# Edge scores of a graph network on one core: target rows spread by one-hot products in a new stage before the scoring stage, part of the source rows gathered there

## The chip, the core and the metric

The kernel runs on one core of a Trainium2 chip. The metric is the time of one launch on the device in microseconds (us). The core has a matrix engine (TensorE, PE; its weight loads are listed apart as PEld), a vector engine (VectorE, DVE), a scalar engine (ScalarE, ACT), a general engine (GpSimd, POOL), a sequencer that only issues transfers (SyncE, SP), and 16 DMA engines that all queues share.

## The reference, cut to what matters

x has 50,000 nodes of 128 values; there are 50,000 edges with a source and a target. The edges are sorted by target; sources are random. Four graph layers follow one another, each with a residual and a layer norm. The change is in the fourth:

```python
q = (node_features @ Wq.T + bq).reshape(N, H, D)
k = (node_features @ Wk.T + bk).reshape(N, H, D)
v = (node_features @ Wv.T + bv).reshape(N, H, D)
scores = jnp.sum(q[src] * k[dest], axis=-1) / jnp.sqrt(jnp.float32(D))
scores = scores + attention_mask
seg_max = jax.ops.segment_max(scores, src, num_segments=N)
ex = jnp.exp(scores - seg_max[src])
seg_sum = jax.ops.segment_sum(ex, src, num_segments=N)
weights = ex / seg_sum[src]
weighted = v[src] * weights[:, :, None]
out = jax.ops.segment_sum(weighted, dest, num_segments=N)
```

## The kernel before, in words

Nodes and edges are cut into 392 tiles of 128 rows each, and these into 98 groups of four tiles (Q = 4). A table of a group in HBM is 256 KB. `program` runs the stages one behind the other, with a barrier of all engines between them (`end_phase`, L63): `setup` (L68), the edge MLP, an aggregation `agg0`, `normalise_project`, the aggregations `agg1` to `agg4` (of which `agg1` to `agg3` run node work beside them), `project_normalise`, then `edge_scores` (L1645), `softmax_by_source` (L1978), `agg5` and a last `project_normalise`.

**An aggregation** (`aggregate`, L269) adds the rows of edges into the rows of their targets. Since edges are sorted by target, it walks 784 steps (node tiles and edge tiles merged), four steps to a quad, 196 quads. For each quad VectorE makes four one-hot tiles in one instruction (L450), and TensorE multiplies each with a tile of edge rows into a bank of PSUM (L520); ScalarE empties a finished bank (L562, L564), fills it with its start values (L551, L553) and stores it. The numbers of steps at which buffers come free are worked out in `setup` and read into registers as the stage runs.

**agg1** has `MeanProducts` (L651) beside it: for each finished group its sums are read back and TensorE transposes them (`turn`, L722) and multiplies them with two weights (`products`, L731 to L737). VectorE's step for a group (L772) does first `keep` of the group four before (L758: copy of the first product, L763: second product plus a residual), then `copy` of the group two before (L770: transposed rows from PSUM). TensorE's `turn` of a group waits for that copy, since there are two transposed buffers.

**edge_scores** handles one group of 512 edges at a time:

- POOL gathers four tiles of source rows and four of target rows of `x3` (`gather`, L1718, one indirect DMA of 128 rows of 512 B at L1737 for each tile), and three groups later scatters four tiles of scores by source (`scatter`, L1742, L1748). It also copies indices (L1716). These are 12 indirect DMAs for a group, all issued in order by POOL.
- TensorE transposes the eight tiles (`turn`, L1776 and L1777), transposes the group's one-hot rows (`lean`, L1786), starts the products of the previous group with their biases (L1808, L1809), then for each of four tiles looks up a place in the order of sources (`look_up`, L1797 and L1798) and does the products of the previous group (L1812, L1813); at last it counts (L1819).
- ScalarE rounds the table of places (L1859), copies the transposed source rows from PSUM (L1852), copies the transposed one-hot rows (`copy_lo`, L1866) and keeps two products of the previous group (L1875, L1876).
- VectorE copies the transposed target rows from PSUM (`copy_target`, L1911), forms the rest of the rounding (L1939), then in turns a rank (L1945) and the selection from the looked up row (L1950) for each of the four tiles, writes the places (L1954 to L1960), scores the previous group (L1916 to L1924) and makes the one-hot rows of the next group (`make_hot`, eight instructions at L1932 and L1933).
- SP loads a row of 512 source numbers, broadcast to 128 partitions (L1696), and stores the group's values (L1701).

The look-up of a tile waits for the selection of the tile before (L1796), and the selection waits for the look-up (L1949), so that the two engines hand over to each other four times in a group. The order of the work on each engine is the order in its `body`.

## Time and profile before

| | |
|---|---|
| median of 3 runs | 7013.81 us (7011.34 to 7027.35) |
| the profiled execution | 7010.85 us |
| its span, first to last instruction | 7009.2 us |
| mean granted TensorE clock, share of full | 0.793 |
| instructions | 133354 |
| moved by DMA | 1119.21 MB |

A row of the view of windows gives for a stretch the busy time of each engine with its count of instructions, the granted clock, the mean busy share of the 16 DMA engines and the rate in GB/s. A row of the view of groups gives line, engine, operation, output and input, count, busy time and mean ns of one, then the time that the engine was idle before them and what ended that. A fp32 matmul of this kernel stands in the trace as two MATMUL records.

### The profile page before, as it was taken

To read this page: it belongs to the slowest core of one execution; us is meant where nothing else is said; L and a number is where in the kernel's file an instruction comes from. 1 tells how busy PE (TensorE), PEld (TensorE's weight loads), DVE (VectorE), ACT (ScalarE), POOL (GpSimd) and SP (SyncE) were. 2 spreads that over 40 slices of the span, in tenths; PEclk is the share of its full clock that TensorE was granted. 3 is DMA by queue.
4 is the path that set the end of the run, shared out by engine and by line. 5 is a ranking of instruction groups with operands and counts; after the bars stand their busy time and mean duration, and the time that the engine had idled before them with its cause. 6 is when DMAs were issued, how large, how long until landed. Compare 5 with 4: busy or idle time off the path is not lost. (4 is left out here: it accounts for less than half of the span.)

```text
span 7009.2 us, 133354 instructions
## 1 busy us (share of the span) xinstructions
PE 4774.6 (68%) x26165; PEld 3739.8 (53%) x26166; DVE 4285.0 (61%) x13848; ACT 2451.2 (35%) x6084; POOL 4258.3 (61%) x4642
## 2 busy tenths in 40 slices
PE   3666666778868876546887767666666666346557
PEld 2555555557757765435764555444444444235545
DVE  4555556887635543863556757866666666665458
ACT  1555555325652125205313416711111111122149
POOL 3777773003575557667776775477777777347730
PEclk7777777999989988558999967977777777667579
DMA  1222223658969976976875536722222222123358
GB/s 29 72 75 73 74 73 110 196 168 297 342 207 302 314 253 210 343 247 207 268 227 180 179 96 232 248 74 69 70 72 69 69 72 69 49 81 115 85 181 289
DMA packets 616834, 1119.21 MB, mean 160 GB/s; under 512 B 124786, under 2 KB 133392, under 8 KB 616336
## 3 DMA queue, kind: packets, MB, share of 16 engines
q1 hardware_dynamic: 299984, 547.66, 23.3%
q10 hardware_dynamic: 183456, 334.05, 13.8%
q0 software_dynamic: 133280, 236.29, 12.7%
q8 instruction: 34, 0.56, 0.0%
q14 instruction: 80, 0.66, 0.0%
HBM read 675.98 MB, written 441.55 MB: 159 GB/s over the span
## 5 line engine op out<-in xcount | busy, mean ns | idle before, releaser
L520 PE MATMUL agg_bank<-agg_msgs,agg_onehot 128*128 x7840 | 1344.0, 325 | 541.9 <-DVE agg_onehot L450 423.6
L520 PEld LDWEIGHTS agg_bank<-agg_msgs,agg_onehot 128*128 128x128 f32 x7840 | 1161.7, 227 | 777.2 <-issue 773.1
L450 DVE TENSOR_TENSOR agg_onehot<-iota,rel 128x512 f32<-128x512 f32 x1176 | 809.9, 689 | 706.6 <-PE agg_bank L520 271.3
L368 POOL DMA_INDIRECT agg_msgs<-near,agg_rows x784 | 792.7, 1011 | 375.3 <-issue 205.5
L368 POOL DMA_INDIRECT agg_msgs<-y,agg_rows x784 | 784.6, 1001 | 261.6 <-issue 200.4
L564 ACT ACTIVATE agg_kept<-agg_bank 128x512 f32<-128x512 f32 x294 | 175.6, 597 | 1097.9 <-PE agg_bank L520 1084.0
L365 POOL DMA_INDIRECT agg_weight<-weights,agg_rows x392 | 410.7, 1048 | 124.4 <-issue 103.0
L520 PE MATMUL agg_bank<-agg_weighted,agg_onehot 128*128 x1568 | 339.5, 387 | 209.9 <-DVE agg_onehot L450 161.8
L1452 POOL DMA_INDIRECT mlp_xs<-in_x,mlp_rows x392 | 409.2, 1044 | 116.7 <-issue 115.8
L562 ACT ACTIVATE agg_kept<-agg_bank,inv_root 128x128 f32<-128x128 f32 x784 | 224.1, 369 | 721.2 <-PE agg_bank L520 672.1
L1748 POOL DMA_INDIRECT by_source<-score_line,score_places x392 | 389.3, 993 | 125.6 <-issue 117.4
L1060 POOL TENSOR_SCALAR l_o<-l_z,l_rstd,l_shift 128x128 f32<-128x128 f32 x196 | 85.7, 440 | 610.8 <-DVE l_shift L1105 608.4
L1776 PE MATMUL score_pSrc<-ident,score_xs 128*128 128x128 f32 x392 | 149.8, 392 | 449.9 <-issue 326.6
L1452 POOL DMA_INDIRECT mlp_xd<-in_x,mlp_rows x392 | 385.7, 984 | 116.0 <-issue 112.1
L1737 POOL DMA_INDIRECT score_xd<-x,score_rows x392 | 384.6, 981 | 116.1 <-issue 116.1
L1737 POOL DMA_INDIRECT score_xs<-x,score_rows x392 | 380.0, 969 | 116.6 <-issue 110.5
L520 PEld LDWEIGHTS agg_bank<-agg_weighted,agg_onehot 128*128 128x128 f32 x1568 | 294.1, 281 | 255.8 <-issue 255.8
L1950 DVE CUSTOM_DVE_ANT_0 score_look_sink<-score_look,score_hot_hi 128x392 f32<-128x392 f32 x392 | 222.1, 567 | 270.6 <-PE score_look L1798 268.3
L1472 PE MATMUL mlp_pSrc<-ident,mlp_xs 128*128 128x128 f32 x392 | 140.1, 372 | 342.4 <-DMA mlp_xd<-in_x,mlp_rows 296.5
L1776 PEld LDWEIGHTS score_pSrc<-ident,score_xs 128*128 128x128 f32 x392 | 77.6, 198 | 485.1 <-issue 485.0
L1812 PE MATMUL score_pQV<-score_w_qv,score_xsT 128*128 128x256 f32 x784 | 333.3, 519 | 0.0
L527 PE MATMUL agg_counts<-agg_hot_hi,agg_hot_lo 128*128 128x392 bf16 x784 | 216.9, 362 | 150.0 <-issue 77.3
(344 smaller groups left out, 11942.3 us busy)
## 6 DMA issues: line engine op xcount, KB each, us to landing
sums<-agg_kept ACTq DMA_DIRECT2D x490, 256.0 KB
agg_first<-start ACTq DMA_DIRECT2D x196, 256.0 KB
agg_first<-y ACTq DMA_DIRECT2D x196, 256.0 KB
messages<-mlp_m SPq DMA_DIRECT2D x98, 256.0 KB, 2.1
agg_first<-in_x ACTq DMA_DIRECT2D x98, 256.0 KB
agg_msgs<-messages SPq DMA_DIRECT2D x98, 256.0 KB
l_z<-sums SPq DMA_DIRECT2D x98, 256.0 KB
x<-l_o POOLq DMA_DIRECT2D x98, 256.0 KB
```

The costliest lines, as they stand in the source:

```text
L365: pool.indirect_dma_start(weight[:, j, :], None, weights[:, :], bass.IndirectOffsetOnAxis(ap=rows[:, third, j:j + 1], axis=0)).then_inc(sm ...
L368: pool.indirect_dma_start(msgs[:, j, :], None, table[:, :], bass.IndirectOffsetOnAxis(ap=rows[:, third, j:j + 1], axis=0)).then_inc(sm[f"g ...
L450: nc.vector.tensor_tensor(onehot[:, j, :, :], k.iota[:, 0:P].unsqueeze(1).to_broadcast([P, Q, P]), k.rel[:, ds(i * (4 * Q) + j * Q, Q)].un ...
L520: t.matmul(bank[:, column[q], :], onehot[:, j, q, :], messages[:, slot[q], :], start=False, stop=True, skip_group_check=True)\
L527: last = t.matmul(counts[:, 0:NT], hot_lo[:, j, w, :], hot_hi[:, j, w, :], start=False, stop=True, skip_group_check=True)
L562: last = a.activation(kept[:, u, q, :], bank[:, u * Q + q, :], ACT.Relu if floor else ACT.Copy, scale=scale[:, ds(g * Q + q, 1)])
L1452: pool.indirect_dma_start(to[:, b, q, :], None, x[:, :], bass.IndirectOffsetOnAxis(ap=rows[:, half, which, at + q:at + q + 1], axis=0)).th ...
L1737: pool.indirect_dma_start(to[:, b, q, :], None, x3[:, :], bass.IndirectOffsetOnAxis(ap=rows[:, half, which, at + q:at + q + 1], axis=0)).t ...
L1748: pool.indirect_dma_start(by_source[:, :], bass.IndirectOffsetOnAxis(ap=places[:, b, q:q + 1], axis=0), line[:, b, q, :], None).then_inc(s ...
L1776: t.transpose(pSrc[:, q, :], xs[:, u, q, :], k.ident[:, :])
L1812: t.matmul(pQV[:, q, :], xsT[:, u % 2, q, :], w_qv[:, :], start=False, stop=True, skip_group_check=True)
L1950: v.tensor_tensor_reduce(out=look_sink[:, q, :], in0=look[:, 0:NT], in1=hot_hi[:, u % 2, q, :], scale=1.0, scalar=0.0, op0=ALU.mult, op1=A ...
```

## The change

`setup` also transposes the table of each step's relative edge targets and writes it to HBM as bf16 rows (seven transposes, two copies, one DMA).

A new stage `spread_rows` runs before `edge_scores`. It walks the same 196 quads as an aggregation, the other way round: SP loads node tiles of `x3` in order (98 loads of 256 KB), VectorE compares the broadcast relative rows with the partition's number to make the one-hot tiles, TensorE multiplies them with the node tiles, so that each edge gets its target's row, and ScalarE empties each finished group of edges, clears the bank and stores 256 KB to `target_rows`. POOL issues 49 broadcast loads of the relative rows (one for four quads, 512 KB each, two buffers) and, between them, gathers the source rows of every fourth group (24 groups, 96 indirect DMAs) and stores them to `source_rows`.

In `edge_scores` SP loads the target rows of each group from `target_rows`, and the source rows of each fourth group from `source_rows`; POOL gathers sources for the other three only, and no targets. The copy of the transposed target rows moves from VectorE to ScalarE, behind the copy of the source rows.

In `MeanProducts` VectorE's `copy` (lag 2) moves ahead of `keep` (lag 4).

The diff, cut to its core and with its indentation shortened:

```diff
+    sp.wait_ge(sm["rel_rows"], 2)
+    sp.dma_start(rel_rows.rearrange("a (j s e) -> s (a j) e", s=REL_ROWS, e=P), relT[:, :, :]).then_inc(sm["rel_out"], 16)
+    sp.wait_ge(sm["rel_out"], 16)
...
+    dve.wait_ge(sm["turned_rel"], STEPS // REL_ROWS)
+    v.tensor_copy(relT[:, 0:4, :], pT[0:REL_ROWS, :, :]).then_inc(sm["rel_rows"], 1)
+    v.tensor_copy(relT[:, 4:7, :], pHT[0:REL_ROWS, 0:3, :]).then_inc(sm["rel_rows"], 1)
...
+    pe.wait_ge(sm["pe_ready"], 6)
+    for j in range(STEPS // REL_ROWS):
+        to = pT[0:REL_ROWS, j, :] if j < 4 else pHT[0:REL_ROWS, j - 4, :]
+        t.transpose(to, k.rel[:, j * REL_ROWS:(j + 1) * REL_ROWS], k.ident[:, :]).then_inc(sm["turned_rel"], 1)
...
-for lag, what in ((4, keep), (2, copy)):
+for lag, what in ((2, copy), (4, keep)):
...
+def spread_rows(nc, k, table, rel_rows, out, ahead):
+
+    ROUNDS = (GROUPS - BANKS) // BANKS
...
+        nodes = sb("nodes", [P, RING, C])
+        rel = sb("rel", [P, 2, CHUNK, Q * P], BF16)
+        onehot = sb("onehot", [P, CHUNK, Q, P])
+        kept = sb("kept", [P, BANKS, Q, C])
+        zero = sb("zero", [P, Q, C])
+        rows, got = sb("rows", [P, 2, Q], I32), sb("got", [P, 2, Q, C])
+        bank = ctx.enter_context(nc.psum_tensor("spread_bank", [P, BANKS * Q, C], F32))
...
+    def store(i, m):
+        pool.wait_ge(sm[f"moved{m}"], i * (16 * Q) + 16 * Q)
+        pool.dma_start(rows_of(ahead, i * (2 * DEEP) + (m * DEEP + DEEP - 1)), got[:, m, :, :]).then_inc(sm[f"kept{m}"], 16)
+
+    def gather(i, m):
+        if not isinstance(i, int) or i > 0:
+            pool.wait_ge(sm[f"kept{m}"], i * 16)
+        pool.sem_inc(sm["pass_pool"], 1)
+        pool.wait_ge(sm["rows"], i * 2 + (m + 1))
+        pool.sem_inc(sm["pass_pool"], 1)
+        for q in range(Q):
+            pool.indirect_dma_start(got[:, m, q, :], None, table[:, :], bass.IndirectOffsetOnAxis(
+                ap=rows[:, m, q:q + 1], axis=0)).then_inc(sm[f"moved{m}"], 16)
+
+    def chunk(i, c):
+        if not isinstance(i, int) or i * CHUNK + c >= 2:
+            pool.wait_ge(sm["onehot"], i * (CHUNK * CHUNK) + (c - 1) * CHUNK)
+        pool.sem_inc(sm["pass_pool"], 1)
+        pool.dma_start(rel[:, c % 2, :, :], rel_rows[:, ds(i * (CHUNK * CHUNK * Q * P) + c * (CHUNK * Q * P), CHUNK * Q * P)]
+                       .to_broadcast([P, CHUNK * Q * P])).then_inc(sm[f"rel{c % 2}"], 16)
+
+    def body(i):
+        for c in range(CHUNK):
+            chunk(i, c)
+            if c % 2 == 0:
+                copy_rows(i, c // 2)
+            else:
+                gather(i, c // 2)
+                if c == 3:
+                    store(i, 0)
+                elif not isinstance(i, int) or i > 0:
+                    store(i - 1, 1)
...
+    def load(i, u):
+        g = i * DEEP + u
+        sp.wait_ge(sm["summed"], sp.value_load(k.node_left[0:1, ds(g, 1)], min_val=1, max_val=STEPS + SHIFT))
+        sp.dma_start(nodes[:, u * Q:(u + 1) * Q, :], rows_of(table, g)).then_inc(sm[f"loaded{u}"], 16)
+
+    def arrive(i, u):
+        sp.wait_ge(sm[f"loaded{u}"], i * 16 + 16)
+        sp.sem_inc(sm["arrived"], 1)
+
+    def body(i, u):
+        for lag, step in ((0, load), (2, arrive)):
+            if live(*before_by(i, u, lag)):
+                step(*before_by(i, u, lag))
+
+    rounds(sp, body, 2)
...
+        dve.wait_ge(sm[f"rel{c}"], i * 16 + 16)
+        for j in range(CHUNK):
+            at = i * (2 * CHUNK) + (c * CHUNK + j)
+            ready = dve.snap(least[0], min_val=1, max_val=ET)
+            arrived = dve.snap(least[1], min_val=1, max_val=GROUPS)
+            dve.sem_inc(sm["pass_dve"], 1)
+            dve.wait_ge(sm["arrived"], arrived)
+            dve.sem_inc(sm["pass_dve"], 1)
+            dve.wait_ge(sm["ready"], ready)
+            dve.sem_inc(sm["pass_dve"], 1)
+            dve.wait_ge(sm["summed"], i * (2 * CHUNK * Q) + ((c * CHUNK + j) * Q + 1))
+            nc.vector.tensor_scalar(onehot[:, j, :, :], rel[:, c, j, :].rearrange("p (q e) -> p q e", q=Q), k.pid[:, 0:1], None, ALU.is_equal)\
+              .then_inc(sm["onehot"], 1)
+            read_needs(ds(at + 1, 1))
...
+    with pe.Fori(0, CHUNKS) as i:
+        for j in range(CHUNK):
+            column = [pe.snap(r, min_val=0, max_val=BANKS * Q - 1) for r in regs[0:Q]]
+            slot = [pe.snap(r, min_val=0, max_val=RING - 1) for r in regs[Q:2 * Q]]
+            pe.wait_ge(sm["onehot"], i * CHUNK + (j + 1))
+            for q in range(Q):
+                t.matmul(bank[:, column[q], :], onehot[:, j, q, :], nodes[:, slot[q], :], start=False, stop=True, skip_group_check=True)\
+                 .then_inc(sm["summed"], 1)
+            for half in (0, Q):
+                pe.reg_load(regs[half:half + Q], k.places[0:1, ds(i * CHUNK + (j + 1), 1), half:half + Q])
...
+        act.wait_ge(sm["summed"], act.value_load(k.edge_done[0:1, ds(g, 1)], min_val=1, max_val=STEPS + SHIFT))
+        a.activation(kept[:, u, :, :], bank[:, u * Q:(u + 1) * Q, :], ACT.Copy).then_inc(sm["emptied"], 1)
+        act.wait_ge(sm["emptied"], g + 1)
+        if not isinstance(i, int) or g + BANKS < GROUPS:
+            fill(u)
+        act.dma_start(rows_of(out, g), kept[:, u, :, :]).then_inc(sm[f"written{u}"], 16)
...
+    def load_rows(i, u):
+        g = i * DEEP + u
+        if after(i, u, DEEP):
+            sp.wait_ge(sm["turned"], g - (DEEP - 1))
+            sp.sem_inc(sm["pass_sp"], 1)
+        sp.dma_start(xd[:, u, :, :], rows_of(target_rows, g)).then_inc(sm[f"dst{u}"], 16)
+        if u == DEEP - 1:
+            sp.dma_start(xs[:, u, :, :], rows_of(source_rows, g)).then_inc(sm[f"src{u}"], 16)
...
-        for lag, step in ((0, load_sources), (3, store)):
+        for lag, step in ((0, load_rows), (0, load_sources), (3, store)):
...
-        for which, to, sem in ((0, xs, "src"), (1, xd, "dst")):
-            for q in range(Q):
-                pool.indirect_dma_start(to[:, b, q, :], None, x3[:, :], bass.IndirectOffsetOnAxis(
-                    ap=rows[:, half, which, at + q:at + q + 1], axis=0)).then_inc(sm[f"{sem}{b}"], 16)
-                if q == 1 and to_copy:
-                    copy_rows(g + 2, 1 - half, which, to_copy)
+                was, place = before_by(i, u, DEEP, TWICE)
+                if live(was, place, TWICE):
+                    pool.wait_ge(sm[f"src{b}"], (was * 2 + place // DEEP) * (16 * Q) + 16 * Q)
+                    pool.sem_inc(sm["pass_pool"], 1)
+        for q in range(Q):
+            pool.indirect_dma_start(xs[:, b, q, :], None, x3[:, :], bass.IndirectOffsetOnAxis(
+                ap=rows[:, half, at + q:at + q + 1], axis=0)).then_inc(sm[f"src{b}"], 16)
+            if q == 1 and to_copy:
+                copy_rows(g + 2, 1 - half, to_copy)
...
-            if live(*before_by(i, u, lag, TWICE), TWICE):
+            if live(*before_by(i, u, lag, TWICE), TWICE) and (lag or u % DEEP < DEEP - 1):
...
-        pe.wait_ge(sm[f"src{u}"], i * (16 * Q) + 16 * Q)
-        pe.wait_ge(sm[f"dst{u}"], i * (16 * Q) + 16 * Q)
+        pe.wait_ge(sm[f"src{u}"], i * (16 * Q) + 16 * Q if u < DEEP - 1 else i * 16 + 16)
+        pe.wait_ge(sm[f"dst{u}"], i * 16 + 16)
...
+        a.activation(xdT[:, u % 2, :, :], pDst[:, :, :], ACT.Copy).then_inc(sm["copied_dst"], 1)
...
-    def copy_target(i, u):
-        g = i * DEEP + u
-        dve.wait_ge(sm["turned"], g + 1)
-        if after(i, u, 2):
-            dve.wait_ge(sm["product"], g - 1)
-        v.tensor_copy(xdT[:, u % 2, :, :], pDst[:, :, :]).then_inc(sm["copied_dst"], 1)
...
+        spread_rows(nc, k, x3, rel_rows, target_rows, source_rows)
+        edge_scores(nc, k, ins, x3, source_rows, target_rows, values, by_source)
```

## Rows read from the trace of the kernel before

**Rows 1.** The page's first part: busy time and share of each engine over the span.
```profile
PE 4774.6 (68%) x26165; PEld 3739.8 (53%) x26166; DVE 4285.0 (61%) x13848; ACT 2451.2 (35%) x6084; POOL 4258.3 (61%) x4642
```

**Rows 2.** Windows: agg0, normalise_project, the middle of agg1, edge_scores.
```profile
1187.00:1604.00 417.00, 310.06 (x1959) 214.72 (x1960) 346.33 (x980) 115.52 (x194) 0.00 (x0) 0.99 0.57 180
...
1620.00:1880.00 260.00, 257.64 (x1948) 219.82 (x1949) 196.42 (x1046) 197.30 (x474) 134.60 (x287) 0.98 1.00 371
2200.00:2500.00 300.00, 263.30 (x1981) 226.50 (x1980) 177.15 (x275) 41.82 (x122) 169.53 (x181) 1.00 0.95 315
...
4531.00:6056.00 1525.00, 1031.11 (x4215) 716.89 (x4215) 968.78 (x3251) 253.06 (x490) 1164.16 (x1226) 0.72 0.25 71
```

**Rows 3.** Groups by line, edge_scores, 4700 to 5900 us.
```profile
L1748 POOL DMA_INDIRECT by_source<-score_line,score_places x310 | 307.9, 993 | 94.5 <-issue 88.4 <-DVE score_line L1924 6.1
L1737 POOL DMA_INDIRECT score_xd<-x,score_rows x310 | 303.9, 980 | 91.8 <-issue 91.8
L1737 POOL DMA_INDIRECT score_xs<-x,score_rows x312 | 302.3, 969 | 92.4 <-issue 88.1 <-PE score_pDst L1777 4.3
...
L1933 DVE TENSOR_SCALAR score_hot_hi<-iota,src_hi 128x392 bf16<-128x392 f32 x308 | 140.1, 455 | 0.0
```

**Rows 4.** Waits, edge_scores, 4700 to 5900 us: total us, times, longest us.
```profile
DVE score_xdT L1911 <- PE score_pDst L1777: 150.1, 69, 3.6
```

**Rows 5.** Timeline of VectorE, one group: start us, duration us, instruction, idle before.
```profile
5008.84 0.62 DVE L1933 TENSOR_SCALAR score_hot_hi<-iota,src_hi 128x392 bf16<-128x392 f32 x1
5009.38 0.67 DVE L1911 COPY score_xdT<-score_pDst 128x512 f32<-128x512 f32 x1
...
5012.25 0.57 DVE L1950 CUSTOM_DVE_ANT_0 score_look_sink<-score_look,score_hot_hi 128x392 f32<-128x392 f32 x1 [1.47 <-PE score_look L1798]
...
5014.18 0.57 DVE L1950 CUSTOM_DVE_ANT_0 score_look_sink<-score_look,score_hot_hi 128x392 f32<-128x392 f32 x1 [0.95 <-PE score_look L1798]
...
5016.12 0.57 DVE L1950 CUSTOM_DVE_ANT_0 score_look_sink<-score_look,score_hot_hi 128x392 f32<-128x392 f32 x1 [0.82 <-PE score_look L1798]
...
5017.34 0.57 DVE L1950 CUSTOM_DVE_ANT_0 score_look_sink<-score_look,score_hot_hi 128x392 f32<-128x392 f32 x1
...
5022.85 0.58 DVE L1933 TENSOR_SCALAR score_hot_hi<-iota,src_hi 128x392 bf16<-128x392 f32 x1
5026.17 0.69 DVE L1911 COPY score_xdT<-score_pDst 128x512 f32<-128x512 f32 x1 [2.74 <-PE score_pDst L1777]
```

**Rows 6.** Windows of 4 us in the same group: the clock is the third number from the end.
```profile
5012.00:5016.00 4.00, 4.00 (x14) 3.17 (x14) 2.09 (x8) 0.00 (x0) 2.93 (x4) 0.50 0.17 49
...
5020.00:5024.00 4.00, 0.00 (x0) 0.00 (x0) 3.24 (x11) 0.00 (x0) 3.08 (x4) 0.91 0.58 168
```

**Rows 7.** Timeline: TensorE's weight loads for one quad, in agg5.
```profile
6331.12 0.97 PEld L520 LDWEIGHTS agg_bank<-agg_weighted,agg_onehot 128*128 128x128 f32 x8 [0.35 <-issue]
```

**Rows 8.** Groups by line and form: VectorE in agg0, and at the start of edge_scores.
```profile
L461 DVE TENSOR_SCALAR agg_hot_hi<-iota,dst_hi 128x392 bf16<-128x392 f32 x392 | 163.7, 418 | 0.0
...
L1899 DVE TENSOR_SCALAR score_earlier<-iota,score_rank 128x512 f32<-128x512 f32 x4 | 1.9, 486 | 0.1
```

**Rows 9.** DMA issues: KB each, median us to landing; and one line's issue cost on POOL.
```profile
score_src_row<-in_src_rows SPq DMA_DIRECT2D x98, 256.0 KB, 4.0
...
L1067 POOL DMA_DIRECT2D x<-l_o x95 | 55.1, 580 | 0.0
```

**Rows 10.** agg1: timeline of one transpose on TensorE, and the wait's total, 2200 to 2500 us.
```profile
2306.47 0.66 PE L722 MATMUL l1p_pT<-ident,l1p_h 128*128 128x128 f32 x4 [0.49 <-DVE l1p_hT L770]
...
PE l1p_pT L722 <- DVE l1p_hT L770: 36.5, 69, 0.7
```

**Rows 11.** Timeline: VectorE's last two instructions of setup.
```profile
93.32 1.16 DVE L239 SCALAR_TENSOR_TENSOR rel<-ns,pN 128x392 f32<-128x392 f32 x2 [8.86 <-PE pN L265]
```

**Rows 12.** The join before agg0: the MLP's last work, and agg0's first quad.
```profile
1176.09 1.28 ACT L1561 ACTIVATE mlp_m<-mlp_h,ew 128x128 f32<-128x128 f32 x4 [0.28 <-DVE mlp_h L1628]
...
1187.44 1.78 PEld L520 LDWEIGHTS agg_bank<-agg_msgs,agg_onehot 128*128 128x128 f32 x8 [5.41 <-issue]
```

117 lines of the change are left out of this document (98 added, 19 removed).

## The prediction

> **What bounds the kernel now.** I read the page's first part first: over the whole span no engine is full, PE is busy 68%, POOL and DVE 61% each [rows 1]. These are averages over stages with different limits, so the view of windows comes next, one row for each stage that the change touches [rows 2]. edge_scores lasts 1525 us; POOL is busy 1164 us of it, DVE 969, PE 1031 at a clock of 0.72, and the DMA engines a quarter. The view of groups tells what POOL does there: three kinds of indirect DMA of 0.97 to 0.99 us, each with about 0.30 us of issue before it and almost no wait for another engine [rows 3]. Twelve in a group make 12 x 1.28 = 15.4 us, and 98 x 15.4 = 1509 us: POOL's queue paces this stage.
>
> The question is then what is next behind POOL. The view of waits says that DVE waits for the transposed targets 150 us in 1200, which is 1.9 us for each of the 78 groups [rows 4]. So POOL is late by little. The timeline of DVE shows it in one group [rows 5]. Take as the mark the end of the last one-hot instruction. It falls at 5009.46 (5008.84 + 0.62). The gathers were early here: the copy of the targets follows at once. The mark of the next group falls at 5023.43 (5022.85 + 0.58). This group took 13.97 us with no delay by POOL in it. Behind that mark the gathers are late: DVE idles 2.74 us. So POOL's pace of 15.4 stands over a chain between DVE and PE of about 13.9 us. That chain has three parts: 2.8 us from the mark to the first selection (5012.25), 5.1 us from the first to the fourth selection (5017.34), 6.1 us to the next mark. In the middle part PE is busy without a gap at a granted clock of 0.50, and selections come 1.93 us apart; the last comes 1.22 us behind its predecessor, when the clock has risen. In the last part PE does nothing for 4 us [rows 5, 6].
>
> **The change part by part.** All sums are against the profiled execution (7010.85 us), 3 us under the median shown.
>
> Scoring stage. POOL keeps 3 gathers on average and 4 scatters, 7 x 1.28 = 9.0 us a group, well under the chain. It no longer sets the pace. The chain of 13.9 remains. The copy of the targets leaves DVE (0.67 us), but it stood in the first part, where DVE idles 1.47 us afterwards for PE's look-up: only the idle time grows, and I count nothing. If PE's clock were full there, that cover would be thinner, and up to 0.6 us of it would show. The same copy on ACT costs 0.6 us; ACT is free then, since the transposes now come right behind the counting and some 3 us before the mark. The one-hot instructions get a little shorter: 455 ns beside a busy POOL [rows 3], 418 ns beside an idle one [rows 8]; with the small one of each pair some 0.2 us a group at most, of which I take 0.1, as POOL is still busy two thirds of the time. That makes 13.8 us. SP's queue gets one or two loads of 256 KB for a group, ahead of the source numbers and the store. Their waits are for events three groups back, so I count nothing; the DMA share of 0.25 leaves room. Without that cover each late load would stop the transposes for its landing, 4.0 us for one of this size [rows 9]. Sum: the stage's time beside its groups is 1525 - 1509 = 16 us; 98 x 13.8 + 16 = 1368, so **-157 us**. Bounds for a group: 13.5 and 14.2, for -186 and -117.
>
> The Trainium skill's page "Advanced Engine Details and Errata" (VectorE Performance Modes) says that POOL's instructions and DVE's two-port modes block each other. By that rule the new stage's one-hot instruction, of such a form and beside gathers, could wait out a POOL instruction. The trace shows 37 ns of such a cost in a mean of 455 [rows 3, 8], so the measurement decides, and I price it by that.
>
> The new stage. It walks 196 quads, with no predecessor in the trace; four resources bound it. PE: eight weight loads for a quad take 0.97 us, with 0.35 us of issue ahead where registers are read between quads [rows 7]: 1.32 us, 259 us in all. DVE: one instruction of 512 columns, about 0.49 us [rows 8], and the register reads; not the bound. POOL: for 16 quads 8 gathers of 1.28, four broadcast loads and two stores of 0.58 each [rows 9] and two copies, about 14 us, or 0.9 a quad. DMA: relative rows 49 x 512 KB, nodes in and edge rows out 98 x 256 KB each, gathers in and out 6.3 MB each, 89.7 MB together; at 371 GB/s, the rate of the stage whose DMA share is 1.00 [rows 2], 242 us. Three of these bounds are close to each other (259, 242, 176), and each load of relative rows has one chunk of four quads to land in, while POOL stands in four gathers half of the time. So it won't reach the highest of them. The nearest thing measured is agg0, same skeleton without gathers: 417 us, 2.13 a quad, but there DVE is busy 83% with five instructions [rows 2]. I take 1.45, nearer to PE's bound than to agg0, since DVE has one instruction in place of five. 196 x 1.45 = 284. Between stages lie some 10 us from the last work to the first quad [rows 12], and at the end stores land and engines meet; I add 20 for both: **+304 us**. Bounds: 242 + 20 = 262, and agg0's pace, 417 + 20 = 437.
>
> Setup. After the last instructions, which end at 94.5 us [rows 11], there now come seven transposes, two copies of about 0.7 us and a DMA of 200 KB whose landing is waited for, 2 to 4 us: **+7 us**, bounds 4 and 12.
>
> agg1. In its middle a step takes 300 / 69 = 4.35 us, and PE waits 0.5 us in each for DVE's copy, which stands behind `keep`, which in turn waits for PE's products [rows 10]. With the copy first that wait has no cause. What is late next is DMA: its share is already 0.95 at 315 GB/s [rows 2], and the highest share of rows 2 is 1.00. So a gain of 5% of the 420 us in which this pattern holds, not 0.5 / 4.35 of it: **-21 us**, bounds 0 and -45.
>
> Sum: -157 + 304 + 7 - 21 = +133, and 7010.85 + 133 = **7143 us**. The gathers that go cost less than they look: they stood over a chain that is nearly as long.
>
> **The rivals.**
>
> *The clock stays up (faster).* In the scoring stage PE waits less for data, so it could hold full speed through the look-ups. For it: the clock does rise within the look-ups, and a selection then follows after 1.22 us. Against: 4 us of idle PE in each group come from DVE's scoring and one-hot instructions, not from POOL, and they stay; the group of rows 5, which had no wait for POOL, ran its look-ups at 0.50. Price: the middle part falls from 5.1 to about 4.1 us (1.4 for each of three), the first part from 2.8 to about 1.9, so 98 x 1.9 = 186 us less: 6957 us. It decides if the granted clock of the stage goes above 0.95. The Trainium skill's page "TensorE: Matmul & The Clock Gate" (HAM oscillation) has the rule: idle gaps bring the clock back to half, and work packed without gaps keeps it up. By that rule fewer waits for gathers speak for this rival and the remaining gap against it.
>
> *The new stage goes at the pace of its relative rows (slower still).* One load of 512 KB can start only when the one-hots of the chunk before last are done. From there to the next such point lie its issue (0.6), its landing and four one-hots with their register reads (about 3.2). With two chunks in flight, 8 quads at 1.45 are 11.6 us, so it decides where landing takes over 7.8 us; half that size lands in 4.0 with the DMA engines a quarter busy [rows 9], and the gathers and a store can put up to 5.8 us in front. Price: 1.8 us a quad, 196 x 0.35 = 69 us more, 7212 us; at agg0's pace 7276.
>
> *Scoring is no shorter.* If SP's in-order queue holds back the loads, or another chain sets in at 15.4 us, nothing of the 157 comes: 7300 us. Nothing in the waits speaks for it.
>
> **How the numbers follow.** My forecast gets 0.62, the relative rows 0.21, the clock 0.10, scoring no shorter 0.04; 0.03 is left for a small miss towards no change. A measurement of this kernel can tell about 0.3% (21 us) from no change. The bounds of the forecast itself: the low ends together make -186 + 262 + 4 - 45 = +35, the high ends -117 + 437 + 12 = +332. Not all ends come together, so the range goes from 7050 to 7270, which leaves out the clock rival, the last one, and the far end of the second. Faster has the clock rival and a little more, 0.11; within 0.3% 0.03; slower 0.86.
>
> **What the profile after would show.** Right: a new stretch of about 300 us before edge_scores with the clock near 1.00, DMA share over 0.85, PE busy about 80%; edge_scores at 1370 us with POOL busy some 50% and waits of POOL for PE or DVE, selections still 1.9 us apart at a clock of 0.50, DVE idle before the first selection up by 0.6 us; agg1's middle at 4.1 us a step and no wait of PE for the copy at L770's place. Wrong: groups of edge_scores under 12.5 us would break the chain that I put at 13.9; DVE waits for relative rows in the new stage, and quads of over 1.7 us, would move me to the second rival; under 1.2 us a quad the issue time that I counted for PE was hidden.

## The result, and the profile after

| | before | changed |
|---|---|---|
| median, runs on one chip | 7012.58 us (4 runs) | 7288.88 us (7287.15 to 7290.68, 4 runs) |
| ratio | | 1.0387, 95% interval 1.0373 to 1.0401 |
| span of the profiled execution | 7009.2 us | 7289.0 us |
| instructions | 133354 | 142209 |
| moved by DMA | 1119.21 MB | 1209.10 MB |

The changed kernel is 3.9% slower. The forecast was 7143 us with 7050 to 7270 as its range: right in its direction, 146 us too low, and above the range.

The account needs the length of each stage. I take it from barrier to barrier (the instruction of `clear_and_free_semaphores` that ends each stage). Stages that are not listed moved by 4 us or less each.

| stage, us | before | changed | difference | predicted |
|---|---|---|---|---|
| setup | 95.0 | 102.4 | +7.4 | +7 |
| agg1 | 662.1 | 658.0 | -4.1 | -21 |
| new stage | | 445.3 | +445.3 | +304 |
| edge_scores | 1533.4 | 1360.7 | -172.7 | -157 |
| all others | 4718.7 | 4722.6 | +3.9 | 0 |
| sum | 7009.2 | 7289.0 | +279.8 | +133 |

Of the miss of 147 us, 141 lie in the new stage. The gain of the change, 173 us, came as forecast, and 16 us more; agg1 gave 17 us less than forecast, and it is luck that these two cancel.

The view of windows of the changed kernel, for the middle of agg1, the new stage and edge_scores (columns as in [rows 2]):
```profile
2200.00:2500.00 300.00, 281.15 (x2043) 236.94 (x2042) 174.87 (x281) 44.02 (x128) 171.08 (x185) 0.99 0.97 324
4530.00:4985.00 455.00, 301.09 (x1572) 261.36 (x1572) 101.22 (x211) 119.84 (x203) 143.38 (x197) 0.77 0.63 200
4985.00:6340.00 1355.00, 953.56 (x4215) 648.00 (x4215) 886.03 (x3140) 306.87 (x588) 688.62 (x710) 0.75 0.26 79
```
In the new stage nothing is full: PE 66%, POOL 32%, VectorE 22%, the DMA engines 0.63 at 200 GB/s. A stage where nothing is full waits in turns, or is paced by something that is not counted as busy. The waits of the stage:
```profile
ACT spread_kept L1819 <- PE spread_bank L1802: 314.0, 98, 8.6
POOL spread_rel L1709 <- DVE spread_onehot L1774: 240.5, 45, 10.5
PEld spread_bank L1802 <- issue: 176.6, 170, 6.2
DVE spread_onehot L1774 <- PE spread_bank L1802: 160.5, 102, 4.1
DVE spread_onehot L1774 <- SPq L1742: 97.0, 49, 4.3
...
PE spread_bank L1802 <- DVE spread_onehot L1774: 58.0, 51, 5.3
DVE spread_onehot L1774 <- ACT spread_bank L1812: 57.7, 28, 4.3
...
DVE spread_onehot L1774 <- DMA spread_rel<-rel_rows: 5.9, 1, 5.9
```
Three readings. ACT, POOL and DVE all wait, and most of their waits lead to PE: ACT waits for it, POOL for DVE, and DVE more for PE (160.5 us) than for SyncE's report (97.0) or ACT (57.7). PE waits 58.0 us for DVE's one-hot tiles, but its weight loads wait 176.6 us for "issue", which is no other engine. The relative rows were late once, for 5.9 us: the rival that had them set the pace is refuted. The groups of the stage give the prices:
```profile
L1774 DVE TENSOR_SCALAR spread_onehot<-spread_rel,pid 128x512 f32<-128x512 bf16 x196 | 97.4, 497 | 337.6 <-PE spread_bank L1802 160.5 <-SPq L1742 97.0 <-ACT spread_bank L1812 57.7
...
L1709 POOL DMA_DIRECT2D spread_rel<-rel_rows x47 | 26.0, 553 | 241.4 <-DVE spread_onehot L1774 240.5 <-issue 1.0
```
The one-hot instruction takes 0.497 us (0.49 priced), so it doesn't wait out POOL's gathers, and POOL's issue of a broadcast load takes 0.553 (0.58 priced). These were right.

**What fills "issue".** The timeline of the weight loads, in the changed kernel (start, duration of the eight loads of a quad, idle time before them in brackets):
```profile
4704.84 1.69 PEld L1802 LDWEIGHTS spread_bank<-spread_nodes,spread_onehot 128*128 128x128 f32 x8 [0.97 <-issue]
4706.74 1.74 PEld L1802 LDWEIGHTS spread_bank<-spread_nodes,spread_onehot 128*128 128x128 f32 x8 [0.21 <-issue]
4709.19 0.97 PEld L1802 LDWEIGHTS spread_bank<-spread_nodes,spread_onehot 128*128 128x128 f32 x8 [0.71 <-issue]
```
From start to start lie 1.90 and 2.45 us. At 4706.74 the idle time is only 0.21, because the eight loads before it took 1.69 us, at a granted clock of 0.66 in that stretch (4704 to 4707 us); at the full clock they take 0.97, and at 0.50 1.78 (e10 below, 4702 to 4704 us). So the idle time shrinks when the loads are slow, and the distance of the starts does not. The trace also has the records of PE's own sequencer, the part that issues its instructions, which the profile doesn't count as busy (start us, us, line, instruction; same stretch, the weight loads between them left out):
```
4707.10 0.074  L1802 FUSED_REGOPS    (last of four matmuls with addresses from registers)
4707.25 0.051  L1805 FUSED_REGOPS
4707.36 0.335  L1805 TENSOR_LOAD     (slots' registers: four values)
4707.75 0.051  L1805 FUSED_REGOPS
4707.86 0.914  L1805 TENSOR_LOAD     (columns' registers: four values)
4708.83 0.173  L1798 FUSED_REGOPS
```
Between two quads the sequencer issues four matmuls, about 0.16 us apart, and then two loads of registers one behind the other, each 0.50 us from start to start where it isn't held up (the second one here is). That makes 4 x 0.16 + 2 x 0.50 + 0.23 for the addresses of the next quad = 1.87 us. Over the stage's 195 distances between quads 5% are under 1.85 us, a quarter under 1.87, half under 2.10, and the mean is 2.22. Every fourth distance has a turn of the loop in it; of these half are under 2.56 us, so a turn adds about 0.68 us. A floor of 196 x 1.87 + 49 x 0.68 = 400 us is thus the stream of instructions itself; 196 x 2.22 = 435 leaves 35 us for waits, and 10 us are the joins.

### The profile page after: what moved, and what is told of

It is laid out like the page before. It is cut to its first block and busy times, and to the rows that moved or that the text cites. A ratio compares the mean times of both kernels' runs of the same rounds, so it can differ in the third digit from the quotient of the medians.

```text
span 7289.0 us, 142209 instructions
## 1 busy us (share of the span) xinstructions
PE 5019.4 (69%) x27744; PEld 3939.5 (54%) x27745; DVE 4299.5 (59%) x13952; ACT 2620.4 (36%) x6378; POOL 3924.8 (54%) x4322
## 2 busy tenths in 40 slices
DMA packets 659861, 1209.10 MB, mean 166 GB/s; under 512 B 125570, under 2 KB 134176, under 8 KB 659360
## 5 line engine op out<-in xcount | busy, mean ns | idle before, releaser
L1802 PE MATMUL spread_bank<-spread_nodes,spread_onehot 128*128 x1568 | 299.2, 354 | 140.0 <-issue 80.4
L1802 PEld LDWEIGHTS spread_bank<-spread_nodes,spread_onehot 128*128 128x128 f32 x1568 | 260.9, 252 | 179.0 <-issue 176.6
L1941 POOL DMA_INDIRECT score_xs<-x,score_rows x296 | 289.9, 979 | 87.4 <-issue 86.5
L1989 PE MATMUL score_pLo<-score_ident_b,score_hot_lo 128*128 128x128 bf16 x392 | 59.3, 306 | 374.3 <-DVE score_hot_hi L2130 374.3
```

The costliest lines, as they stand in the source:

```text
L1802: t.matmul(bank[:, column[q], :], onehot[:, j, q, :], nodes[:, slot[q], :], start=False, stop=True, skip_group_check=True)\
L1941: pool.indirect_dma_start(xs[:, b, q, :], None, x3[:, :], bass.IndirectOffsetOnAxis(ap=rows[:, half, at + q:at + q + 1], axis=0)).then_inc ...
```

## The experiments

Theory A: TensorE's sequencer paces the new stage by its loads of registers. Rivals: the gathers or the DMA traffic in the stage; the report of arrived rows by SyncE; the banks; the clock, which is 0.77 in the stage. For edge_scores: the chain of 13.7 us is what remains, and the clock sets its length.

The runs went in five sessions, each with its own runs of the kernel before. In two of them (e1 to e4, and e9 to e12) it takes 7011 to 7019 us, as above; in three (e5 to e8, f1 to f4, and f5 and f6) it takes 8258 to 8276 us. I call these the first and the second kind of session. The expectations speak of chips like the first and like the second, but that the chip makes the difference isn't shown: the record has the chips 6 and 3 for the first kind, and 12, 15 and again 6 for the second. The new stage is alike in both: 445.3, 443.1, 441.4 and 442.1 us in the first, 443.7 and 443.7 in the second, where nothing in it was changed.

**One load instead of two (e1).**
```diff
-for half in (0, Q):
-    pe.reg_load(regs[half:half + Q], k.places[0:1, ds(i * CHUNK + (j + 1), 1), half:half + Q])
+pe.reg_load(regs, k.places[0:1, ds(i * CHUNK + (j + 1), 1), 0:2 * Q])
```


> The changed kernel, but TensorE's sequencer reads the eight place registers of the next quad with one load in place of two of four. Theory A (the new stage goes at the pace of TensorE's sequencer: between the matmuls of two quads it makes two register loads of about 0.5 us each, in series): the quad of 2.2 us gets shorter by up to 0.5 us where nothing else is late, the stage of 445 us goes to 350 to 400. Theory B (the pace is set by VectorE's own waits and register load): under 10 us less. Theory C (DMA or relative rows): no change.

Measured: 7239.23 us; the new stage 392.8 us, 52.5 less; edge_scores 1360.3. The weight loads of e1:
```profile
4703.97 0.97 PEld L1802 LDWEIGHTS spread_bank<-spread_nodes,spread_onehot 128*128 128x128 f32 x8 [1.16 <-issue]
4705.73 0.97 PEld L1802 LDWEIGHTS spread_bank<-spread_nodes,spread_onehot 128*128 128x128 f32 x8 [0.79 <-issue]
4707.37 0.97 PEld L1802 LDWEIGHTS spread_bank<-spread_nodes,spread_onehot 128*128 128x128 f32 x8 [0.67 <-issue]
```
A quarter of the distances are now under 1.64 us, 5% under 1.60, some 0.24 less: one load of eight registers stands 0.76 us in the stream, two of four 1.00. A turn of the loop adds 0.49 us where it added 0.68. Together that is 196 x 0.24 + 49 x 0.19 = 56 us, near the 52.5 measured. Nothing else in the stage was touched.

**Twice the loads (e2), then four loads of two registers (e10, and e5).** In e2 each load stood twice, with `for half in (0, Q, 0, Q)`.

> The changed kernel with each of the two register loads on TensorE made twice (same values). Theory A: 1.0 us more for each quad, the stage goes from 445 to about 620 to 645 us, and nothing else moves. Theories B and C: TensorE has slack of its own, so less than half of that: under 540 us.

Measured: 7297.02 us, the stage 443.1. The trace still has two TENSOR_LOADs for a quad: 394 in the stage, as many as in the changed kernel. The repeated loads, which had no effect on any value, are not among the records. The run tells nothing of theory A. The next one keeps every load alive:
```diff
-for half in (0, Q):
-    pe.reg_load(regs[half:half + Q], ...)
+for part in range(0, 2 * Q, 2):
+    pe.reg_load(regs[part:part + 2], k.places[0:1, ds(i * CHUNK + (j + 1), 1), part:part + 2])
```


> The changed kernel, with the eight registers of a quad (four slots, four columns) fetched on TensorE in the new stage by four loads of two registers in place of two loads of four; the same eight values, none of them left out. Theory A (TensorE's own instruction stream paces the stage, and loads of registers are served one after the other at about 0.5 us each, whatever their size): two further loads, 196 x 2 x 0.5 = about +195 us if every one lay on the path, +150 to +195 us since some 45 us of the stage are other waits that a longer period covers; the new stage at about 600 to 640 us where it was 445.3, the whole at about 7440 to 7485 us. Theory B (loads are served by bytes, or the idle of the weight loads comes from the one-hot products, the banks or the rows): the new stage stays at 445 +- 10 us. All other stages unchanged in both.

> Four loads of two registers in the new stage, beside the changed kernel on one chip this time (e5 stood alone on its chip). Theory A (TensorE's instruction stream paces the stage): e5 showed a shortest period of 3.70 us a quad where the changed kernel has 1.87; 196 x 3.7 + 49 x 0.5 = 750 us, so the stage at 740 to 790 us on either chip, +300 to +330 us. Rival B (loads are not on the path and e5's stage was long by its chip): the stage within 20 us of the changed kernel's on the same chip.

Measured: the stage takes 789.9 us in e5 (second kind) and 790.9 in e10 (first kind; the whole 7630.57 us against 7287.62 for the changed kernel in the same session). The weight loads of e10:
```profile
4702.02 1.78 PEld L1802 LDWEIGHTS spread_bank<-spread_nodes,spread_onehot 128*128 128x128 f32 x8 [1.91 <-issue]
4705.72 1.78 PEld L1802 LDWEIGHTS spread_bank<-spread_nodes,spread_onehot 128*128 128x128 f32 x8 [1.92 <-issue]
4710.05 1.78 PEld L1802 LDWEIGHTS spread_bank<-spread_nodes,spread_onehot 128*128 128x128 f32 x8 [2.55 <-issue]
```
The distance is 3.70 us. Each load of two registers stands 0.71 us in the stream: 4 x 0.71 - 2 x 0.50 = 1.84, and 3.70 - 1.87 = 1.83. The granted clock also fell, to 0.50 in e10's stage (0.77 in the changed kernel's, 0.89 in e1's), but it doesn't set the distance: the eight weight loads end 1.78 us after their start, and the records of the four register loads fill the stream up to 3.34 us after it. With e1, this shows theory A: the same eight registers, in one, two or four loads, and the stage follows the number of loads in both directions, by 0.24 and 1.83 us a quad. My price of 0.5 us for each further load was too low, and the expectation of e5 (600 to 640 us) with it.

**No gathers in the stage (e3).** All source rows are gathered in edge_scores; POOL's `copy_rows`, `gather` and `store` are gone from the new stage.

> The changed kernel without the gathers and stores of source rows in the new stage; all source rows are gathered by POOL in the scoring stage (8 indirect DMAs a group, 10.2 us of POOL). Theory A: the new stage stays within 10 us of 445, since POOL isn't late in it. Theory C (POOL's gathers delay the relative rows or crowd the DMA engines): it gets shorter by 30 us or more. The scoring stage stays at 1361 us within 10, since its chain of 13.66 us a group is above POOL's 10.2.

Measured: 7283.42 us; the new stage 438.2, edge_scores 1362.2. The quarter of the gathers costs 3 to 7 us where it stands (the stage takes 441.4 to 445.3 us with them in this kind of session), and it costs 1 or 2 us in edge_scores: moving it was neither a gain nor the cause.

**Fillers for TensorE in edge_scores (e4).** Twelve records of matmul work whose result nobody reads fill the gap before the one-hot transposes:
```diff
+def fill_gap(i, u):
+    g = i * DEEP + u
+    if after(i, u, 1):
+        pe.wait_ge(sm["selected"], g * Q)
+        for _ in range(FILLERS):
+            t.matmul(look[:, 0:2 * C], w_k[:, :], w_qv[:, :], start=True, stop=True)
...
     turn(*now)
+    fill_gap(*now)
     lean(*now)
```


> The changed kernel with six matmuls of fixed operands (256 columns, results never used) in TensorE's idle gap of each scoring group, before it waits for the one-hot rows. Theory A (the chain of a group is 13.66 us because the clock falls in that gap and most look-ups run at half of it): granted clock of the stage above 0.9, selections 1.4 us apart, a group 11.9 to 12.3 us, the stage 1170 to 1210 us in place of 1361. Rival (the chain is set by the engines' hand-overs whatever the clock, or the filler delays the look-ups): 1340 us or more.

Measured: 7106.05 us; edge_scores 1177.5, 183 less; the new stage 441.4. The window of edge_scores in e4:
```profile
5000.00:6100.00 1100.00, 979.07 (x5176) 728.99 (x5175) 844.49 (x3002) 294.87 (x566) 661.67 (x675) 0.94 0.31 92
```
DVE's waits for the look-ups, first in the changed kernel (5200 to 6200 us), then in e4 (5200 to 6000 us):
```profile
DVE score_look_sink L2147 <- PE score_look L2001: 265.4, 220, 2.1
```
```profile
DVE score_look_sink L2156 <- PE score_look L2009: 117.9, 169, 1.2
```
The granted clock is 0.94 where the changed kernel has 0.75, and a wait for a look-up takes 0.70 us on average where it took 1.21. For a group that is 1.7 us of waiting (117.9 over the 68 groups of the window) where it was 3.6 (265.4 over 73), and 98 x 1.9 = 186 us is about what the stage lost. This is the clock rival of the prediction, priced at 186 us there. Its size was right; it doesn't come by itself, since the gap that DVE's work leaves in PE stays. The Trainium skill's page "TensorE: Matmul & The Clock Gate" (HAM oscillation) says that idle gaps bring the clock down and closely packed work keeps it up; this trace agrees, with 0.75 and 0.94.

**The report of arrived rows (e6, e11, f2).** SyncE reports a group's rows two groups behind their load, and that report stands behind the next load's wait. All three runs have e1's one load.
```diff
-for lag, step in ((0, load), (2, arrive)):
+for lag, step in ((1, arrive), (0, load)):      # e6, e11
+for lag, step in ((2, arrive), (0, load)):      # f2
```


> The changed kernel with one load of eight registers in the new stage, and SyncE's step that reports a group of relative rows as arrived put ahead of the step that starts the next load (with a lag of one group, where it was two groups behind it). Theory A1 (after the one load, a part of the new stage's 392.8 us is VectorE's wait for that report, 97.0 us of idle time before the one-hot products in the changed kernel, since the report stands behind the next load's own wait): the stage falls to about 355 to 380 us. Rival (the idle time of VectorE is not on the path, since TensorE's stream paces all): 393 +- 5 us. Other stages as in the run with one load.

> One load of eight registers in the new stage and the report of arrived rows ahead of the next load, beside the changed kernel on one chip. If that report was on the path after the one load (392.8 us on the first chip): 355 to 380 us on a chip like the first. If not: 393 +- 6 us. On a chip like the second, 459.5 us as in e6, whatever the report costs.

> One load of eight registers in the new stage, and the report of two groups before put ahead of the load (two loads stay in flight, and the report no longer stands behind the load's wait for a free slot). If the late report is what is left over the instruction stream's floor (e1: 392.8 us, shortest period 1.60 us: 196 x 1.62 + 49 x 0.49 = 342 us): 345 to 380 us. If VectorE's waits there are shadows of the banks and of TensorE: 388 to 398 us. If the loads come too late by it, as in e11: over 400 us.

Measured: 459.5 us for the stage in e6 and 461.8 in e11, against 392.8 with the old order; 387.7 in f2. The waits of e11's new stage:
```profile
DVE spread_onehot L1774 <- SPq L1742: 151.4, 48, 5.4
DVE spread_onehot L1774 <- PE spread_bank L1802: 150.6, 110, 3.6
```
In e1 the first of these is 82.7 us. With the report one group behind and ahead of the load, SyncE waits for a landing before it issues the next load, so one load is in flight and not two: the wait that I wanted to shorten grew. That one load is in flight is read from the order of the code; f2, which differs from e6 in the lag alone, doesn't have the loss. With two groups behind (f2) the stage is 5 us shorter than e1's, hardly more than the 4 us by which the same stage differs between runs: the waits for the report fall from 82.7 to 38.9 us, and in their place come waits of DVE for PE, 192.1 us for 141.9 in e1. So of the idle time that the profile puts down to the report nearly all that went was time in which DVE would have waited for something else.

**One load of registers in the kernel before (e7, f3).** The same edit in `read_places` of the aggregations, nothing else.

> The kernel before, with one load of eight registers in place of two of four in the aggregation's TensorE loop (five stages of 196 quads and the first one, nothing else changed). Theory A (the same stream of instructions stands in the aggregations, at 2.2 to 3.4 us a quad): where a quad is paced by it, up to 0.27 us a quad (52.5 / 196, what the new stage gained) or 52 us a stage; the first aggregation (432.7 us, 2.2 us a quad) should give most, 20 to 50 us, the others 0 to 20 us each since other engines pace their longer steps; sum 7013 - 40 to - 130, or 6885 to 6975 us. Rival (the aggregations are paced by the rows, the one-hot products and the weighted messages alone): 7013 +- 10 us.

> The kernel before with one load of eight registers in the aggregations' TensorE loop. In e12 the first aggregation fell from 431 to 383.7 us and the others from 653.7, 596.5, 572.3, 536.2, 558.4 to 646.7, 587.5, 568.8, 537.7, 551.2. So: first aggregation -48, the others -25 in sum: 7011 - 73 = 6938 us, ratio 0.988 to 0.992. If it gives nothing where no stage of the change stands: ratio 1.00.

Measured, both in sessions of the second kind: ratio to the kernel before 0.9942 (95% interval 0.9917 to 0.9968) and 0.9925 (0.9892 to 0.9958). agg0 falls from 432.7 us to 382.1 and 382.9 (it is alike in both kinds: 432.4 to 434.6 in e5, e6, f2, f4 and f6, which don't have this edit). DVE is busy 83% in agg0 [rows 2], yet shortening PE's stream shortened it: agg0 was paced by the same stream (a quarter of its distances under 1.90 us before, under 1.64 in e7), and not by DVE. The later aggregations, which are slower than the stream, give too little to tell from their scatter.

**The target copy back on VectorE (f4, f6).**
```diff
-a.activation(xdT[:, u % 2, :, :], pDst[:, :, :], ACT.Copy).then_inc(sm["copied_dst"], 1)
+v.tensor_copy(xdT[:, u % 2, :, :], pDst[:, :, :]).then_inc(sm["copied_dst"], 1)
```


> The changed kernel with the copy of the turned target rows out of PSUM put back from ScalarE to VectorE, ahead of the remainder step. The prediction costed the move at nothing, in either direction, since VectorE waits 2.8 us before its first selection in a group. By it: the scoring stage 1360 +- 12 us. Rival (the copy of 0.69 us is on VectorE's part of the chain, which has just lost it): 98 x 0.69 = +68 us, the stage at about 1428 us.

> The kernel of f4 again. On a chip like the second its scoring stage was 1473.4 us where e5 and e6 had 1470.2 and 1474.6 with the copy on ScalarE, but there the gathered rows pace the stage. On a chip like the first: 1360 +- 12 us if the move costs nothing either way, 1428 us if the copy of 0.69 us lies on VectorE's chain.

Both fell in sessions of the second kind: edge_scores 1473.4 and 1474.4 us, where e5, e6 and f2, with the copy on ScalarE, have 1470.2, 1474.6 and 1474.4. The 68 us of the rival are not there. Since the stage is longer in these sessions, the part of a group that the copy stands in is the better witness. First f4, then the changed kernel, from the last one-hot instruction to the first selection:
```profile
5999.75 0.43 DVE L2136 TENSOR_SCALAR score_hot_hi<-iota,src_hi 128x392 bf16<-128x392 f32 x1
6000.10 0.67 DVE L2114 COPY score_xdT<-score_pDst 128x512 f32<-128x512 f32 x1
...
6003.03 0.57 DVE L2153 CUSTOM_DVE_ANT_0 score_look_sink<-score_look,score_hot_hi 128x392 f32<-128x392 f32 x1 [1.52 <-PE score_look L2001]
```
```profile
5712.38 0.45 DVE L2130 TENSOR_SCALAR score_hot_hi<-iota,src_hi 128x392 bf16<-128x392 f32 x1
...
5715.69 0.57 DVE L2147 CUSTOM_DVE_ANT_0 score_look_sink<-score_look,score_hot_hi 128x392 f32<-128x392 f32 x1 [2.12 <-PE score_look L2001]
```
Mark to selection is 2.85 us (6003.03 - 6000.18) with the copy on DVE and 2.86 without it; the idle time is 1.52 and 2.12. So it is in all 98 groups: the median is 2.86 us in f4, in f2 of the same session, and in the changed kernel.

**Everything together (e8, e12), and with the old report (f1, f5); the changed kernel again (e9).** One load in the new stage and in the aggregations, PE's loop of the new stage unrolled sevenfold (7 turns of 28 quads), and the fillers; e8 and e12 have the report of e6 as well.

> The changed kernel with the single findings put together: one load of eight registers in the new stage and in the aggregations, the report of arrived rows ahead of the next load, TensorE's loop in the new stage unrolled sevenfold (7 turns of 28 quads in place of 49 of 4), and six filler matmuls in each scoring group. If the gains add up: 7288.9 - 183 (fillers) - 52 (one load) - 15 (report) - 42 x 0.5 = 21 (turns of the loop that are gone) - 40 to - 100 (aggregations) = 6920 to 6980 us, below the kernel before by 0.5 to 1.3%. If the new stage has a second pace right under the first (bank and row waits) and the aggregations give nothing: 7288.9 - 183 - 52 = 7054 us, above the kernel before by 0.6%.

> The changed kernel itself, nothing altered, beside the kernel before on one chip: the chip of the runs e5 to e8 ran the kernel before in 8276 us, and there two kernels that hold the change came out below it. If the chip is like the first: 7289 against 7015 us, ratio 1.039. If it is like the second, where the kernel before has a scoring stage of 2080 us (1533 on the first) because its gathered rows arrive later and later than they are needed: the changed kernel's scoring stage at about 1470 us and its new stage at about 460 + 55 = 515 us, the whole at about 8150 to 8200 us, below the kernel before by 1 to 1.5%; so the sign of the change would hang on how fast the indirect gathers land.

> All the findings together (one load of eight registers in the new stage and the aggregations, the report first, TensorE's loop of the new stage unrolled sevenfold, six fillers in each scoring group). On a chip like the first: 7289 - 183 - 52 - 50 (first aggregation, 432.7 to 382.1 us in e7) - 0 to 40 = 6964 to 7004 us, ratio 0.993 to 0.999 to the kernel before. On a chip like the second: ratio 0.963 as in e8. If one load in the aggregations gives nothing where they are paced by gathers, the upper end holds.

> The kernel of e12 with SyncE's order in the new stage put back as the change has it (load, then the report of two groups before). e12's new stage took 454.6 us, with the report one group behind and ahead of the load; e1's, with the old order, 392.8. If the new order is what lengthened it (only one load of rows is then in flight): the new stage at 370 to 393 us and the whole at 7053.6 - 62 to - 85 = 6969 to 6992 us, ratio to the kernel before 0.994 to 0.997. If the unrolled loop of TensorE lengthened it: 7050 +- 10 us.

> The kernel of f1 again, for its ratio on a chip like the first. Its new stage took 370.1 us in f1 and the first aggregation 383.2, both stages without gathers by index of their own on the path. On a chip like the first: e12's 7053.6 - (454.6 - 370.1) = 6969 us, ratio 0.993 to 0.995. On a chip like the second: 0.957 as in f1.

| run, kind of session | us | before | ratio, 95% interval | new stage | edge_scores |
|---|---|---|---|---|---|
| e9, first | 7287.62 | 7010.80 | 1.0397 (1.0379 to 1.0414) | 442.1 | 1359.9 |
| e12, first | 7053.61 | 7010.80 | 1.0060 (1.0043 to 1.0077) | 454.6 | 1174.9 |
| e8, second | 7975.43 | 8276.06 | 0.9635 (0.9605 to 0.9666) | 460.8 | 1419.3 |
| f1, second | 7904.01 | 8258.01 | 0.9567 (0.9541 to 0.9592) | 370.1 | 1419.1 |
| f5, second | 7900.12 | 8272.74 | 0.9541 (0.9505 to 0.9576) | 368.6 | 1429.0 |

e12 missed its expectation because of the report, whose harm e11 shows; f1 and f5 have the old one, and their new stage is the shortest of all, 370.1 us in f1, 22.7 under e1's, close to the 42 x 0.49 = 21 us of the loop turns that are gone. The fillers give less in the second kind: edge_scores is 45 to 55 us under f2's 1474.4, where e4 gained 183. In a session of the first kind the kernel of f1 didn't run; e12's time less the difference of the new stage, 7053.6 - (454.6 - 370.1) = 6969 us, is an estimate, 0.6% under the kernel before, and not shown.

## Why the prediction was right and wrong, point by point

- **POOL paces edge_scores; behind it stands a chain of 13.9 us: right.** The sum used 13.8, and over 91 groups the mean is 13.66. The parts were 2.8, 5.1 and 6.1; they are 2.86, 4.80 and 6.00. POOL is busy half of the stage (688.62 of 1355 us), as forecast. The granted clock stayed low, 0.72 before and 0.75 after, so the clock rival (0.10) did not come about; e4 shows that its price of 186 us was right (183 measured, at a clock of 0.94).
- **The copy of the targets costs nothing: right**, by the row that was to tell: DVE's wait before the first selection went from 1.47 [rows 5] to 2.12 us, and f4 has the same time from mark to selection with the copy put back.
- **Setup +7: right** (+7.4).
- **agg1 -21: too much.** It moved by -4.1 us here, and by -1 to -11 in the other runs of the first kind that have the change (651.1 to 660.9 us). The wait of PE for the copy [rows 10] is nearly gone, and the DMA share rose to 0.97 as named; in the same 300 us PE now waits 16.5 us for the rows of `h` to land (0.7 before). The error is in the stretch that the gain was counted for: a step takes 300 / 71 = 4.2 us where 4.1 was forecast for the middle, but the gain was taken for all of 420 us. By tens, the steps behind the first ten take 4.7, 4.4, 4.2, 4.3, 4.3, 4.2, 4.0 and 4.3 us, where all of them took 4.4 before.
- **The new stage +304: wrong, and this is the step that failed.** The text says "eight weight loads for a quad take 0.97 us, with 0.35 us of issue ahead where registers are read between quads [rows 7]: 1.32 us". The 0.35 is not the price of the issue. Its neighbours in the same view of the kernel before show why:
```profile
6325.00 0.97 PEld L520 LDWEIGHTS agg_bank<-agg_weighted,agg_onehot 128*128 128x128 f32 x8 [0.93 <-issue]
6326.98 1.66 PEld L520 LDWEIGHTS agg_bank<-agg_weighted,agg_onehot 128*128 128x128 f32 x8 [1.01 <-issue]
6329.14 1.63 PEld L520 LDWEIGHTS agg_bank<-agg_weighted,agg_onehot 128*128 128x128 f32 x8 [0.50 <-issue]
...
6333.56 0.97 PEld L520 LDWEIGHTS agg_bank<-agg_weighted,agg_onehot 128*128 128x128 f32 x8 [1.47 <-issue]
```
The row that I took starts at 6331.12, 1.98 us behind the one before, and that one ran for 1.63 us at a lower clock, as the windows of the kernel before show (clock third from the end):
```profile
6329.00:6331.00 2.00, 1.82 (x8) 1.63 (x8) 1.29 (x2) 1.17 (x2) 1.70 (x2) 0.61 0.64 202
6331.00:6333.00 2.00, 1.15 (x8) 0.97 (x8) 1.29 (x2) 0.87 (x2) 1.46 (x2) 1.00 0.21 65
```
Every distance of the starts above is 1.98 us or more. The floor was there to be read, 1.98 in agg5 and 1.87 in the new stage, and 1.87 in place of 1.32 alone is 108 us. The loop's turns, 49 x 0.68 = 33 us, had no term in the sum at all. So the pace of 1.45 us a quad, 284 us, stood below what PE's stream allows, 400 us, and 2.22 us a quad, 435 us, were measured. The signs missed with it: clock near 1.00 (0.77), DMA share over 0.85 (0.63), PE busy about 80% (66%).
- **"Nearer to PE's bound than to agg0, since DVE has one instruction in place of five": wrong.** agg0's pace of 2.13 us was named as the upper bound, 437 us for the stage, and the measured 445.3 is just over it. e7 shows why the two are alike: agg0 is paced by the same stream, so having one DVE instruction in place of five bought nothing.
- **Relative rows late (0.21): refuted** by one wait of 5.9 us, although one of its two signs, quads of over 1.7 us, did come. The price of its harder end, "at agg0's pace 7276", came close to the result with the wrong mechanism.
- **What stays open.** After f1 the mean distance is 1.84 us over a floor of 1.62, some 40 us of the stage, in which DVE waits for PE, SyncE and the banks. f2 gives at most some 5 us of it to the report; the rest wasn't taken apart.

## What to carry to other kernels

Where a loop has addresses in registers, the engine's own stream can be its bound while no engine is busy: read the distance from start to start over several turns, and look at whether the work between was slow or fast, before an idle time ahead of an instruction is taken as a price. Of a skeleton that is used again, the measured period is worth more than the period that its busy times would allow, until a run has shown what paces it. Load neighbouring registers in one instruction.

## What the runs showed of the hardware that was not expected

- **Loads of registers on TensorE.** From start to start 0.71 us for two registers, 0.50 for four, 0.76 for eight, in series and not under the next matmuls' issue. The Trainium skill's page "Runtime: NRT & Kernel Launch" (Instruction fetch mechanics) states about 200 ns a register; the page speaks of loads from HBM. By that rule e1 would have gained nothing; it gained 0.24 us a quad, so here the count of loads matters more than that of registers.
- **Repeated register loads are not in the trace** (e2): an experiment that doubles a cost must keep both copies of use, and the trace must show them.
- **Two kinds of sessions.** In the second kind the stages that gather or scatter by index are longer, all but the new stage, and the others are not. In e7 (the kernel before with one load): the MLP 1252.6 us for 1085.0, agg1 811.8 for 662.1, edge_scores 2079.7 for 1533.4; but normalise 285.3 for 285.8, softmax 134.3 for 134.7. The instruction itself is no slower there, as the groups of e7's edge_scores from 5600 to 6400 us show beside [rows 3]:
```profile
L1747 POOL DMA_INDIRECT by_source<-score_line,score_places x146 | 147.7, 1012 | 279.2 <-issue 279.2
L1736 POOL DMA_INDIRECT score_xs<-x,score_rows x148 | 143.0, 966 | 43.8 <-issue 43.8
```
POOL waits beyond its 0.30 us of issue only ahead of the scatters. Nor do the gathers' packets come later: from the issue of a gather of source rows to the end of its last packet lie 2.2 us in both (median of 392, from the records of the DMA queue; 2.15 in the kernel before, 2.21 in e7). What delays these stages wasn't found, nor whether it is the chip. It may turn the sign, though: f4 and f6, one run each of the changed kernel but for one copy, take 8102.84 and 8070.98 us beside 8258.01 and 8272.74 for the kernel before, 1.9% and 2.4% less. The changed kernel itself wasn't run in such a session. There the scoring stage falls from 2079.7 and 2105.3 us (e7 and f3) to 1473.4 (f4), more than the 444 us of the new stage; in the first kind, for which the change was predicted, it falls by 173.
